# Subject products on pairs of tiles in quarters of TensorE, and routing in two batches: a mixture-of-experts kernel

## The chip, the cores and the metric

The kernel runs on one core of one Trainium2 chip. Its time is device microseconds from launch to end. The median of three runs of the kernel before is 865.85 us (863.19 to 867.67). One further execution was taken by the profiler; all rows below are from it.

## The reference

The input x is 64 samples of 64 rows and 512 columns. Each sample has a subject, one of 8.

```python
h = einsum('bct,bcd->bdt', x, weights[subjects]) + bias[subjects][:, :, None]  # 64x64 weights
tokens = h.reshape(4096, 512)
scores = sigmoid(tokens @ gate_weight.T)                  # 16 experts in 4 groups
biased = scores + expert_bias                             # best 2 of 4 groups, then best 4 experts
w = scores[chosen] / sum(scores[chosen]) * 2.5
y = sum over the 4 chosen experts of w * (silu(t @ g.T) * (t @ u.T) @ d.T)
out = x + y + the shared expert's (silu(t @ sg.T) * (t @ su.T) @ sd.T)
```

All is float32: h has 4096 tokens of 512 numbers, an expert 256 hidden units.

## The kernel before, in words

A tile is 128 tokens, that is two samples of 64 rows; there are 32. The program has a front stage and an expert stage. The expert stage runs 175 steps of one tile each: 32 for the shared expert, then 143 for the sorted tokens of the 16 experts. Each engine has its own list of instructions and waits on semaphores.

**The front stage.** ScalarE's queue (line 604) loads the first eight tiles of x into `x_ring`, and SyncE's queue (line 404) the later ones as slots come free; SyncE also stores each h tile to `h_rows` (line 411) and loads the shared expert's weights at tile 8. GpSimd (line 542) reads the two subjects of a tile and copies the two 64x64 weights into the diagonal quarters of a 128x128 block of `cw_ring`, whose other quarters were cleared at the start. TensorE (line 804) multiplies that block with the tile (line 812), then turns the h of the tile before with four transposes (line 768), and for each group of four tiles computes the router's logits in four column tiles of 32 (line 792) and turns them (line 802). The last four tiles' logits are computed directly, each tile in its turn (line 834). ScalarE adds the bias while it copies h out of PSUM (line 639), copies the transposes to a kept place (line 643), applies the sigmoid, and splits the shared weights in a high and a low part (line 620). VectorE routes in batches of eight tiles (`route_groups`, `top_experts`, `chosen_experts`, `count_slots`, `route_weights`): three batches before the expert stage, the fourth in its first steps. For each batch TensorE counts tokens ahead of each token (`positions`, line 771).

**Constants.** GpSimd builds them itself: `late_consts` (line 513) after the weights of tile 4, ending with `lane_q` and `tile_q`, and `clear_pads` (line 529) after tile 10 stores zeros behind `h_rows` and `out` with four DMAs.

**The order in the expert stage** is written out by hand in tables: ROUTE_STEPS says after which shared step VectorE does which part of the routing, ENTRY_STEPS when it builds the entries for the table of slots, PE_POS and PE_POS_FFN when TensorE does `positions`, RAW_LOADS, HIGHS and LOWS when weights are loaded and split, GATHERS when tokens are gathered. TensorE's step (line 920) is gate and up products of tile n, transposes of the hidden part of n - 1, a table or position product if one is due, and the down product of n - 2. At the end ScalarE copies the last three y tiles (line 747), and GpSimd scatters them.

Of the kernel before, what the change touches and what calls it, by code (L numbers as in the profile page):

```python
# [10 lines left out]
ALU = mybir.AluOpType  # L11
# [3 lines left out]
P = 128  # L15
B, C, H = 64, 64, 512
# [9 lines left out]
BC = 8  # L26
NB = NT // BC
BE = BC * E
# [28 lines left out]
ROUTE_STEPS = {0: ("groups",), 1: ("top_experts",), 2: ("ties", "counts"), 3: ("weights",), 4: ("ranks",),  # L57
               5: ("take_turns",), 6: ("starts",), 7: ("slots", "keys"), 8: ("top_slots",), 9: ("places",),
               10: ("words",), 11: ("columns",), 12: ("tables",), 14: ("read_words",), 15: ("read_sp_words",),
               22: ("fill_idx",)}  # L60
ENTRY_STEPS = {9: (0,), 11: (1,), 13: (2, 3), 14: (4,), 15: (5,), 16: (6, 7), 17: (8, 9), 18: (10, 11), 19: (12, 13),
               20: (14, 15)}
N_GROUPS = NT // ENTRIES
PE_POS = {18: 0, 26: 1}
PE_POS_FFN = {1: 2, 3: 3}
PE_WORDS = 13
PE_SP_WORDS = 14
SHARED_LOAD = 8
SHARED_HIGH = {16: 0, 19: 1, 22: 2}
PAD_STORES = 10  # L70
PAIR_TABLES = 4
# [3 lines left out]
HIGHS = {17: (1, 0), 18: (1, 1), 19: (1, 2), 24: (2, 0), 28: (2, 1), 31: (2, 2)}  # L75
# [7 lines left out]
FIRST_X_COPY = 30  # L83
# [21 lines left out]


def scored_by(tiles):

    if tiles <= DIRECT:
        return tiles // LOGIT_TILES  # L110
    return LOGIT_GROUPS + tiles - DIRECT
# [17 lines left out]
def build(nc, x, itok, fside, cond_w, gate_w, expert_bias, ffn_w, out):  # L129
# [4 lines left out]
    with ExitStack() as ctx:  # L134
# [80 lines left out]
        mask = in_raw([P, NB, NG + BC, E])  # L215
# [8 lines left out]
        ties = [in_raw([P, BC, BC + E]) for k in range(3)]  # L224
        top_ties = sb("top_ties", [P, BC, TOPK])
        n_ties = sb("n_ties", [P, BC])
        cum_part = [in_raw([P, NG + BC, E]) for k in range(2)]
# [72 lines left out]
        x_in = [sem(f"x_in{s}") for s in range(RING)]  # L300
# [71 lines left out]

        def shared_tile(n):

            return (n - KEPT_IN_X) % NT
# [10 lines left out]

        block = ctx.enter_context(nc.Block())

        @block.sync
        def _(sp):  # L390

            sp.dma_start(itok_row[:], itok.unsqueeze(0)).then_inc(itok_loaded, 16)
# [6 lines left out]
            def load_x(n):  # L399
                t = tile_at(n)  # L400
                sp.wait_ge(cond_done, t.done(1 - RING))
                sp.dma_start(x_ring[:, t.slot, :], rows(t, x_rows)).then_inc(x_in[t.slot], 16)

            for n in range(NT):
                t = tile_at(n)
                if n + RING < NT:
                    load_x(n + RING)
                if n == SHARED_LOAD:
                    sp.dma_start(raw_w[:, 0:EW], ffn_w[E]).then_inc(shared_loaded, 16)
                sp.wait_ge(h_ready, n + 1)  # L410
                sp.dma_start(rows(t, h_rows), tok_ring[:, t.slot, 0:H]).then_inc(h_stored[t.slot], 16)
# [81 lines left out]
        def _(pool):  # L493
# [19 lines left out]
            def late_consts():  # L513
# [10 lines left out]
                pool.sem_inc(consts, 1)  # L524
                iota(lane_q[:], [[1, P], [0, DUO]], 0, 0)
# [13 lines left out]
            pool.wait_ge(blank, 4)  # L539
            pool.wait_ge(itok_loaded, 16)  # L540

            for n in range(NT):
                subjects = [pool.value_load(itok_row[0:1, 2 * n + half:2 * n + half + 1]) & (NS - 1)
                            for half in range(2)]
                if n == 0:
                    pool.wait_ge(cond_loaded, 16)
                elif n >= RING:
                    pool.wait_ge(cond_done, n + 1 - RING)
                for half, subject in enumerate(subjects):
                    a, b = half * C, half * C + C  # L550
                    pool.tensor_copy(cw_ring[a:b, n % RING, a:b],
                                     cond_sb[a:b, bass.ds(subject * C, C)]).then_inc(cond_w_ready, 1)
                if n == PAIR_TABLES:
                    pool.wait_ge(cond_w_ready, 2 * (n + 1))
                    late_consts()
                elif n == PAD_STORES:
                    clear_pads()
# [45 lines left out]
        def _(act):  # L603
            for n in range(RING):
                if n == 2:
                    act.wait_ge(cond_loaded, 16)
                act.dma_start(x_ring[:, n, :], rows(tile_at(n), x_rows)).then_inc(x_in[n], 16)
# [24 lines left out]
            for n in range(NT + 2):  # L632
                t = tile_at(n)
                if n < NT:
                    act.wait_ge(cond_done, n + 1)
                    if n >= RING:
                        act.wait_ge(h_stored[t.slot], t.rnd * 16)
                        act.wait_ge(a_xposed, n + 1 - RING)
                    act.activation(tok_ring[:, t.slot, 0:H], psY[n % 2][:], ACT.Identity,
                                   bias=bias_tok[:, n:n + 1]).then_inc(h_ready, 1)  # L640
                if 1 <= n <= NT:
                    act.wait_ge(a_xposed, n)
                    act.activation(kept_xT(n - 1), psT[(n + 1) % 2][:], ACT.Copy).then_inc(a_xT_ready, 1)
# [13 lines left out]
                if n in SHARED_HIGH:  # L657
                    if SHARED_HIGH[n] == 0:
                        act.wait_ge(shared_loaded, 16)
                    split_high(0, SHARED_HIGH[n])  # L660
                elif n == FIRST_X_COPY:
                    copy_x(0)
# [836 lines left out]
```

## Time and profile before

| what | us |
|---|---|
| median of three runs | 865.85 |
| the profiled execution | 861.59 |
| its span, first to last instruction | 859.8 |
| start of the first expert product | 72.1 |
| TensorE busy | 838.1 |
| mean granted clock of TensorE | 0.992 of full |

The profiled execution's time is 1.8 us more than its span. In a view, "busy" is time with at least one instruction running on the engine, PEld is TensorE's loading of weights, and names ending in q are an engine's sequencer or queue.

### The profile page before, as it was taken

What the parts mean: (1) busy time and instruction counts of PE and PEld (TensorE: products, weight loads), DVE (VectorE), ACT (ScalarE), POOL (GpSimd) and SP (SyncE); (2) the same over time, 40 slices, a digit from 0 to 9 for tenths busy, and PEclk for the clock granted to TensorE, in tenths of its full rate; (3) what the DMA queues carried; (4) which work ended last, traced back from release to release, by engine and by line L of the source; (5) the groups of instructions that cost most, each with busy time, mean ns of one, the idle gap of its engine ahead of it and who ended that gap; (6) DMA issues with size and microseconds to landing.
All of it is one profiled execution on the core that took longest, in us unless ns stands there. A gap on an engine that the chain in (4) does not pass through costs nothing.

```text
span 859.8 us, 19571 instructions
## 1 busy us (share of the span) xinstructions
PE 838.1 (97%) x4151; PEld 675.4 (79%) x4152; DVE 485.0 (56%) x1055; ACT 418.1 (49%) x870; POOL 439.2 (51%) x402
## 2 busy tenths in 40 slices
PE   7999999999999999999999999999999999999994
PEld 5568887878888888888888888888887888887883
DVE  1478776564654444664446645756647466464440
ACT  3785355754543334644445444635445355453441
POOL 4430211143556555566665567566564665665433
PEclk8999999999999999999999999999999999999998
DMA  7994767579999999899998999899998999999644
GB/s 246 327 358 142 121 111 210 122 141 294 261 238 256 187 186 186 159 229 282 229 174 173 254 254 221 192 284 207 244 263 197 264 258 220 239 165 202 111 63 63
DMA packets 147097, 179.13 MB, mean 208 GB/s; under 512 B 30858, under 2 KB 104210, under 8 KB 144658
## 3 DMA queue, kind: packets, MB, share of 16 engines
q0 software_dynamic: 37296, 86.95, 50.9%
q1 hardware_dynamic: 108258, 80.45, 34.8%
q10 hardware_dynamic: 1408, 10.49, 3.7%
q14 instruction: 117, 0.96, 0.4%
q8 instruction: 18, 0.29, 0.2%
HBM read 82.52 MB, written 65.04 MB: 172 GB/s over the span
## 4 chain that ended last, share of the span: by engine, by line
PE 89%; issue 3%; ACT 3%; DVE 2%; DMA 1%; POOL 1%; DVEq 0%; ACTq 0%; SPq 0%
PE psGU L884 52%; PE psY L884 26%; PE psH L768 4%; PE psY L812 3%; PE psT L768 1%; DMA x_ring<-x 1%; PE psH L792 1%; ACT x_ring L712 1%; DVE entry L1291 1%; DVE x_ring L1293 1%; POOL out L567 1%; ACT split_w L620 0%; PE psGU L834 0%; ACT xT_hi L630 0%; PE psM L910 0%
## 5 line engine op out<-in xcount | busy, mean ns | idle before, releaser
L884 PE MATMUL psGU<-split_w,xT_hi 128*128 (+1 forms) x1400 | 432.0, 390 | 3.0 <-DVE xT_lo L1316 3.0
L567 POOL DMA_INDIRECT out<-y_ring,idx_all x143 | 234.0, 1636 | 205.0 <-SPq L471 189.2
L884 PEld LDWEIGHTS psGU<-split_w,xT_hi 128*128 128x128 f32 x1400 | 262.2, 188 | 60.2 <-issue 4.2
L884 PE MATMUL psGU<-split_w,xT_lo 128*128 (+1 forms) x700 | 273.4, 391 | 0.0
L884 PE MATMUL psY<-split_w,hidT_hi 128*128 (+1 forms) x700 | 232.5, 413 | 0.2 <-issue 0.2
L727 ACT ACTIVATE aT<-psGU 128x256 f32<-128x256 f32 x175 | 67.1, 384 | 259.4 <-PE psGU L884 259.4
L1316 DVE TENSOR_TENSOR xT_lo<-psT,xT_hi 128x512 fp32r<-128x512 f32 x143 | 98.8, 691 | 144.1 <-ACT xT_hi L630 128.3
L562 POOL DMA_INDIRECT tok_ring<-h_rows,idx_all x143 | 148.2, 1037 | 61.0 <-issue 42.7
L679 ACT ACTIVATE y_ring<-psY 128x512 f32<-128x512 f32 x175 | 103.7, 593 | 120.6 <-PE psY L884 115.2
L884 PEld LDWEIGHTS psGU<-split_w,xT_lo 128*128 128x128 f32 x700 | 131.4, 188 | 27.4
L884 PE MATMUL psY<-split_w,hidT_lo 128*128 (+1 forms) x350 | 137.5, 393 | 0.0
L884 PEld LDWEIGHTS psY<-split_w,hidT_hi 128*128 128x128 f32 x700 | 118.5, 189 | 16.1 <-issue 0.5
L1341 DVE SCALAR_TENSOR_TENSOR aT<-aT,w_ring,psGU 128x256 f32<-128x256 f32 x143 | 67.0, 469 | 87.4 <-ACT aT L727 87.3
L1323 DVE STREAM_TRANSPOSE psT<-x_ring 128x512 f32<-128x512 f32 x143 | 102.5, 717 | 0.0
L575 POOL DMA_DIRECT2D out<-y_ring x32 | 28.4, 902 | 113.6 <-ACT y_ring L679 113.3
L630 ACT ACTIVATE xT_hi<-psT 128x512 fp32r<-128x512 f32 x143 | 84.7, 592 | 1.7 <-DVE psT L1323 1.7
L884 PEld LDWEIGHTS psY<-split_w,hidT_lo 128*128 128x128 f32 x350 | 65.7, 188 | 14.4
L1356 DVE TENSOR_TENSOR split_w<-raw_w,split_w x42 | 51.5, 1227 | 42.4 <-ACT split_w L689 34.7
L1329 DVE TENSOR_TENSOR hidT_lo<-psH,hidT_hi 128x256 fp32r<-128x256 f32 x175 | 72.9, 417 | 1.0 <-ACT hidT_hi L670 1.0
L768 PEld LDWEIGHTS psH<-ident,aT 128*128 128x128 f32 x350 | 48.7, 140 | 24.0 <-DVE aT L1339 1.3
L768 PE MATMUL psH<-ident,aT 128*128 128x128 f32 x350 | 66.6, 271 | 0.5 <-DVE hidT_lo L1329 0.5
L670 ACT ACTIVATE hidT_hi<-psH 128x256 fp32r<-128x256 f32 x175 | 66.3, 379 | 1.4 <-PE psH L768 1.4
(184 smaller groups left out, 459.9 us busy)
## 6 DMA issues: line engine op xcount, KB each, us to landing
x_ring<-tok_ring SPq DMA_DIRECT2D x284, 128.0 KB
raw_w<-ffn_w SPq DMA_DIRECT2D x17, 1536.0 KB, 10.9
h_rows<-tok_ring SPq DMA_DIRECT2D x32, 256.0 KB, 6.8
out<-y_ring POOLq DMA_DIRECT2D x32, 256.0 KB
x_ring<-x SPq DMA_DIRECT2D x24, 256.0 KB, 7.8
tok_ring<-h_rows,idx_all POOLq DMA_INDIRECT x143, 6.4
out<-y_ring,idx_all POOLq DMA_INDIRECT x143
x_ring<-x ACTq DMA_DIRECT2D x8, 256.0 KB, 3.9
```

What stands on the lines that cost most here:

```text
L562: pool.indirect_dma_start(tok_ring[:, r % RING, :], None, h_rows[:, :], bass.IndirectOffsetOnAxis(idx_all[:, r:r + 1], 0)).then_inc(gather ...
L567: pool.indirect_dma_start(out[:, :], bass.IndirectOffsetOnAxis(idx_all[:, r:r + 1], 0), y_ring[:, r % YRING, :], None, compute_op=ALU.add) ...
L630: act.activation(xT_hi[:, t.slot % 2, :], xT, ACT.Copy).then_inc(xhi_ready, 1)
L670: act.activation(hidT_hi[:, t.slot % 2, :], psH[:, 0:I], ACT.Copy).then_inc(hidhi_ready, 1)
L679: act.activation(y_ring[:, s, :], psY[t.slot % 2][:], ACT.Copy).then_inc(y_ready, 1)
L727: act.activation(silu[:, t.slot % 2, :], psGU[t.slot % 2][:, 0:I], ACT.Silu).then_inc(silu_ready, 1)
L768: mm = pe.transpose(dst[:, k * P:(k + 1) * P], src[:, k * P:(k + 1) * P], ident[:])
L884: mm = pe.matmul(dst, a[:, slot, c], w(at + col + k * H), start=(k == 0 and a is high and at == 0), stop=(k == parts - 1 and a is low))
L1316: v.tensor_tensor(xT_lo[:, t.slot % 2, :], xT, xT_hi[:, t.slot % 2, :].bitcast(F32), ALU.subtract).then_inc(xT_ready, 1)
L1323: v.transpose(psT[t.slot % 2][:].rearrange("p (k b j) -> p k j b", k=HK, j=QUADS), x_duo[:, t.slot // DUO_TILES, :, t.slot % DUO_TILES, :] ...
L1329: v.tensor_tensor(hidT_lo[:, t.slot % 2, :], psH[:, 0:I], hidT_hi[:, t.slot % 2, :].bitcast(F32), ALU.subtract).then_inc(hidT_ready, 1)
L1341: ins = v.scalar_tensor_tensor(out=hid[:, half, :], in0=gate, scalar=w_ring[:, w_slot, bass.ds(expert, 1)], in1=up, op0=ALU.mult, op1=ALU. ...
```

## The change

- Tiles are handled in pairs. The four samples of a pair are loaded by two DMAs, samples 4m and 4m+3 into partitions 0 to 63, samples 4m+1 and 4m+2 into 64 to 127, each two slots wide.
- `cw_ring` holds each 64x64 weight once, in its first 64 columns, and is no longer cleared. TensorE does four products of 64 rows by 64 columns per pair, at four positions of its array. Four banks of PSUM take turns for h instead of two.
- VectorE copies the transposes of the first 16 tiles to their kept place; ScalarE those of the last 16.
- Routing has two batches of 16 tiles: the first before the expert stage, the second in shared steps 0 to 5. The running sums get one more stage and 8 columns of cleared lead. ROUTE_STEPS, ENTRY_STEPS, PE_POS, PE_POS_FFN and others move by about one step.
- The direct logits of the last four tiles come one after another behind the loop, with one sigmoid for all.
- The shared weights are loaded at pair 2 (tile 4), and split at pairs 6 to 8.
- `late_consts` comes after pair 7, `lane_q` and `tile_q` (now `entry_consts`) and `clear_pads` after the last pair.
- VectorE copies the third last y tile. The load of the subjects' numbers goes from SyncE's queue to ScalarE's.

```diff
-BC = 8
+BC = 16
+LEAD = 8
-PE_POS = {18: 0, 26: 1}
-PE_POS_FFN = {1: 2, 3: 3}
-SHARED_LOAD = 8
-SHARED_HIGH = {16: 0, 19: 1, 22: 2}
-PAD_STORES = 10
-PAIR_TABLES = 4
+PE_POS = {15: 0}
+PE_POS_FFN = {5: 1}
+SHARED_LOAD = 2
+SHARED_HIGH = {6: 0, 7: 1, 8: 2}
+PAIR_TABLES = 7
+DVE_COPIES = 16
-RAW_LOADS = {14: 1, 15: 2, 23: 3, 31: 4}
-WARM_UP = 12
+RAW_LOADS = {15: 1, 16: 2, 23: 3, 31: 4}
+WARM_UP = 8
-FIRST_X_COPY = 30
+FIRST_X_COPY = 15
...
+        def load_pair(eng, m):
+            at = m % X_PAIRS * 2
+            low, high = x[4 * m:4 * m + 4:3], x[4 * m + 1:4 * m + 3]
+            eng.dma_start(x_ring[0:C, at:at + 2, :], low.rearrange("b c t -> c b t")).then_inc(x_in[m % X_PAIRS], 16)
+            eng.dma_start(x_ring[C:P, at:at + 2, :], high.rearrange("b c t -> c b t")).then_inc(x_in[m % X_PAIRS], 16)
...
+        def h_bank(n):
+            return (psY if n // 2 % 2 == 0 else psGU)[n % 2]
...
+            for m in range(N_PAIRS):
+                if m + X_PAIRS < N_PAIRS:
+                    sp.wait_ge(cond_done, 2 * (m + 1))
+                    load_pair(sp, m + X_PAIRS)
+                if m == SHARED_LOAD:
                     sp.dma_start(raw_w[:, 0:EW], ffn_w[E]).then_inc(shared_loaded, 16)
+                for n in (2 * m, 2 * m + 1):
+                    t = tile_at(n)
+                    sp.wait_ge(h_ready, n + 1)
+                    sp.dma_start(rows(t, h_rows), tok_ring[:, t.slot, 0:H]).then_inc(h_stored[t.slot], 16)
...
+                    for half, subject in enumerate(subjects):
+                        a, b = half * C, half * C + C
+                        pool.tensor_copy(cw_ring[a:b, n % RING, 0:C],
+                                         cond_sb[a:b, bass.ds(subject * C, C)]).then_inc(cond_w_ready, 1)
+                if m == PAIR_TABLES:
+                    pool.wait_ge(cond_w_ready, 4 * (m + 1))
                     late_consts()
+            pool.wait_ge(cond_w_ready, 2 * NT)
+            entry_consts()
+            pool.wait_ge(blank, 3)
+            clear_pads()
...
+            for m in range(N_PAIRS + 1):
+                pair = (2 * m, 2 * m + 1)
+                if m < N_PAIRS:
+                    for n in pair:
+                        copy_h(n)
+                if 2 * m > DVE_COPIES:
+                    for n in pair:
+                        keep_xT(n - 2)
...
+            def cond(m):
+                at = m % X_PAIRS * 2
+                pe.wait_ge(x_in[m % X_PAIRS], (m // X_PAIRS + 1) * 32)
+                if m >= 2:
+                    pe.wait_ge(h_ready, 2 * (m - 1))
+                for k, (n, rows_at, cols_at) in enumerate(((2 * m, 0, 0), (2 * m, C, C), (2 * m + 1, 0, C), (2 * m + 1, C, 0))):
...
+                    mm = pe.matmul(h_bank(n)[cols_at:cols_at + C, :], cw_ring[rows_at:rows_at + C, n % RING, 0:C],
+                                   x_ring[rows_at:rows_at + C, at + n % 2, :], start=True, stop=True,
+                                   tile_position=(rows_at, cols_at))
+                    if k % 2 == 1:
+                        mm.then_inc(cond_done, 1)
...
+            for m in range(N_PAIRS + 1):
+                if m < N_PAIRS:
+                    cond(m)
+                if m == 0:
                     bias()
...
+                if m >= 1:
+                    for n in (2 * m - 2, 2 * m - 1):
+                        turn_h(n)
...
+            for n in range(DIRECT, NT):
+                mm = direct_logits(n)
+            mm.then_inc(logits_done, 1)
...
-            v.memset(cw_ring[:], 0.0).then_inc(blank, 1)
...
+            for n in range(DVE_COPIES):
+                v.wait_ge(a_xposed, n + 1)
+                v.tensor_copy(kept_xT(n), psT[n % 2][:]).then_inc(a_xT_ready, 1)
```

## Rows read from the trace of the kernel before

**Rows 1.** The page's part 1: busy us, share of the span, instructions.

```profile
PE 838.1 (97%) x4151; PEld 675.4 (79%) x4152; DVE 485.0 (56%) x1055; ACT 418.1 (49%) x870; POOL 439.2 (51%) x402
```

**Rows 2.** Waits of TensorE, whole span: us in total, times, longest us.

```profile
PE psY L812 <- issue: 3.7, 1, 3.7
PE psGU L884 <- DVE xT_lo L1316: 3.0, 3, 1.6
...
PE psY L812 <- DMA x_ring<-x: 1.2, 1, 1.2
```

**Rows 3.** Timeline of TensorE: start us, us, line, what; products and transposes of tiles.

```profile
30.98 1.02 PE L812 MATMUL psY<-x_ring,cw_ring 128*128 128x512 f32 x2
31.85 0.60 PE L768 MATMUL psT<-ident,tok_ring 128*128 128x128 f32 x4
32.28 1.02 PE L812 MATMUL psY<-x_ring,cw_ring 128*128 128x512 f32 x2
...
72.10 0.72 PE L884 MATMUL psGU<-split_w,xT_hi 128*128 128x512 f32 x2
```

**Rows 4.** Chain that ended last: a logit group, and one tile's direct logits.

```profile
28.54 1.01 PE psH L792 x32
...
71.19 1.06 PE psGU L834 x8
```

**Rows 5.** Groups of ScalarE, 0 to 72 us: busy us, mean ns, idle before.

```profile
L639 ACT ACTIVATE tok_ring<-psY,bias_tok 128x512 f32<-128x512 f32 x32 | 22.0, 689 | 14.8 <-PE psY L812 12.3 <-issue 1.1
L643 ACT ACTIVATE kept_w<-psT 128x512 f32<-128x512 f32 x24 | 14.3, 595 | 0.3 <-PE psT L768 0.2
...
L620 ACT ACTIVATE split_w<-raw_w 128x1024 fp32r<-128x1024 f32 x3 | 3.2, 1061 | 0.0
L647 ACT ACTIVATE logitsT<-psH 128x128 f32<-128x128 f32 x7 | 1.9, 277 | 2.8 <-PE psH L792 2.7
```

**Rows 6.** Stretches of the front: engines' busy us, TensorE's clock, DMA share, GB/s.

```profile
core 0: us, PE busy (x) PEld busy (x) DVE busy (x) ACT busy (x) POOL busy (x), PEclk, DMA share, GB/s
...
40.00:60.00 20.00, 18.43 (x169) 11.21 (x168) 14.39 (x53) 15.70 (x30) 9.07 (x26) 1.00 1.05 400
...
17.00:23.70 6.70, 6.10 (x40) 3.51 (x41) 0.00 (x0) 1.56 (x3) 3.33 (x13) 0.50 0.36 123
```

**Rows 7.** DMA issues, 0 to 72 us: count, KB each, us to landing.

```profile
x_ring<-x SPq DMA_DIRECT2D x24, 256.0 KB, 7.8
```

**Rows 8.** Timeline of GpSimd: constants, and copies of subject weights.

```profile
9.36 0.29 POOL L515 TENSOR_SCALAR_AFFINE_SELECT before<-ones 128x128 f32<-128x128 f32 x1
...
13.17 1.68 POOL L507 IOTA tile_q<- 128x288 f16 x1
16.98 0.52 POOL L551 COPY cw_ring<-cond_sb 64x64 f32 x2 [2.13 <-issue]
18.00 0.52 POOL L551 COPY cw_ring<-cond_sb 64x64 f32 x2 [0.50 <-issue]
```

**Rows 9.** VectorE: groups by form, then the first batch's first and last operation.

```profile
L967 DVE TENSOR_TENSOR raw_w<-raw_w 128x128 f32<-128x128 f32 x24 | 7.0, 290 | 0.7
...
L1316 DVE TENSOR_TENSOR xT_lo<-x_ring,xT_hi 128x512 fp32r<-128x512 f32 x2 | 1.3, 684 | 0.0
...
L1339 DVE TENSOR_TENSOR aT<-aT,psGU 128x256 f32<-128x256 f32 x32 | 13.3, 417 | 5.7 <-ACT aT L727 5.3
...
32.06 0.29 DVE L967 TENSOR_TENSOR masked<-scores,ebias 128x128 f32<-128x128 f32 x1 [21.31 <-ACT scores L650]
...
41.70 0.23 DVE L1096 TENSOR_SCALAR weights_te<-w_num 128x128 f32<-128x128 f32 x1
```

**Rows 10.** A stretch of the expert stage with 32-partition transfers; columns as in rows 6.

```profile
240.80:242.15 1.35, 1.35 (x8) 1.12 (x7) 1.04 (x2) 0.28 (x1) 0.00 (x0) 1.00 1.20 189
```

**Rows 11.** Timeline of the end: y copy by ScalarE, first of the last three scatters.

```profile
845.68 0.59 ACT L679 ACTIVATE y_ring<-psY 128x512 f32<-128x512 f32 x1
...
846.58 1.56 POOL L567 DMA_INDIRECT out<-y_ring,idx_all  x1 [3.33 <-SPq L471]
```

More of the change, by code:

```diff
@@ L537, in clear_pads @@
                                    ).then_inc(scattered[2 * k + 1], 16)
-            pool.wait_ge(blank, 4)
             pool.wait_ge(itok_loaded, 16)
[L542 to L554, printed above, removed]
+            for m in range(N_PAIRS):
+                for n, first, second in ((2 * m, 4 * m, 4 * m + 1), (2 * m + 1, 4 * m + 3, 4 * m + 2)):
+                    subjects = [pool.value_load(itok_row[0:1, b:b + 1]) & (NS - 1) for b in (first, second)]
+                    if n == 0:
+                        pool.wait_ge(cond_loaded, 16)
+                    elif m >= X_PAIRS:
+                        pool.wait_ge(cond_done, 2 * (m + 1 - X_PAIRS))
+                    for half, subject in enumerate(subjects):
[4 more added lines that the diff above has]
+                    pool.wait_ge(cond_w_ready, 4 * (m + 1))
                     late_consts()
-                elif n == PAD_STORES:
-                    clear_pads()
+            pool.wait_ge(cond_w_ready, 2 * NT)
+            entry_consts()
+            pool.wait_ge(blank, 3)
+            clear_pads()
             def gather(r):
@@ L603, in _ @@
         def _(act):
-            for n in range(RING):
-                if n == 2:
+            act.dma_start(itok_row[:], itok.unsqueeze(0)).then_inc(itok_loaded, 16)
+            for m in range(X_PAIRS):
+                if m == 1:
                     act.wait_ge(cond_loaded, 16)
-                act.dma_start(x_ring[:, n, :], rows(tile_at(n), x_rows)).then_inc(x_in[n], 16)
+                load_pair(act, m)
             act.wait_ge(blank, 2)
@@ new lines, in turn_h, with direct_logits @@
+            def turn_h(n):
+                pe.wait_ge(h_ready, n + 1)
+                if n >= 2:
+                    pe.wait_ge(a_xT_ready, n - 1)
+                transposes(psT[n % 2], tok_ring[:, n % RING, 0:H], HK).then_inc(a_xposed, 1)
+            def direct_logits(n):
+                pe.wait_ge(a_xT_ready, n + 1)
+                at = (n - DIRECT) * E
+                xT = kept_xT(n)
+                for k in range(HK):
+                    mm = pe.matmul(psY[0][:, at:at + E], xT[:, k * P:(k + 1) * P], gate_sb[:, k * Q:k * Q + E],
+                                   start=(k == 0), stop=(k == HK - 1))
+                return mm
@@ L837, in _ @@
-                if n in PE_POS:
-                    positions(PE_POS[n])
+                elif 1 <= g <= LOGIT_GROUPS and phase == 0:
+                    turn_logits(g - 1)
+                if m in PE_POS:
+                    positions(PE_POS[m])
+            for n in range(DIRECT, NT):
+                mm = direct_logits(n)
+            mm.then_inc(logits_done, 1)
             def word_tables():
@@ L1025, in route_groups, with best_groups @@
                 settle()
+            def best_groups(b):
+                four = masked[:].rearrange("p (g j) -> p g j", j=GS)
                 sums = per_chunk(group_sum[:], NG)
@@ L1372, in route_part @@
                         route_groups(NB - 1)
+                    elif part == "best_groups":
+                        best_groups(NB - 1)
                     elif part == "top_experts":
@@ L1431, in step @@
                     next_weights(word)
+            for j in range(PIECES):
+                split_low(0, j)
             route_groups(0)
+            best_groups(0)
             top_experts(0)
```

199 lines of the change are left out of this document (77 added, 122 removed).

## The prediction

> **What bounds the kernel now.** I read the busy times of the page first: TensorE is busy 97% of the span and every other engine about half [rows 1]. The table of waits then tells where TensorE stands still: 3.7 us once before a subject product, 1.2 us for a tile of x, 3.0 us in three waits for VectorE's `xT_lo`, and nothing else of size [rows 2]. So the expert stage from 72.1 us on is TensorE's own work, and the change leaves that work as it is. What it rebuilds is the front stage, 0 to 72.1 us, where the first expert product starts: 8% of the span [rows 3].
>
> In the front three things run side by side. TensorE: in a stretch with no waits a subject product takes 31.85 - 30.98 = 0.87 us and the four transposes of a tile 32.28 - 31.85 = 0.43, so 1.30 a tile [rows 3]; a group of four tiles' logits takes 1.01 [rows 4]. With 0.3 around it, four tiles are 6.5 us. ScalarE: 0.69 for the copy of h, 0.60 for the kept transpose, 1.29 a tile, plus 3.2 us of weight splitting and some 0.5 per four tiles for logits, of which 0.27 is the copy shown [rows 5]; it is as full as TensorE. DMA: from 40 to 60 us the engines are full (share 1.05, 400 GB/s) [rows 6], because x (8.39 MB) comes in, h (8.39 MB) goes out and weights (1.57 MB) and pads (2.13 MB) lie between; a load landed 7.8 us after its issue [rows 7].
>
> The 72.1 us are then: 8.1 until the second tile's product, 31 more tiles at 1.63 = 50.5, the direct logits 4 x about 1.0 = 4 [rows 4], sum 62.6. The other 9.5: GpSimd builds constants from 9.36 to 14.85 and gives the sixth tile's weights only at 16.98, so TensorE waits 3.7 [rows 2, 8]; after that wait its granted clock is 0.50 of full (1.2 instead of 2.4 GHz) from 17.0 to 23.7 [rows 6], which costs about 6.7 / 2 = 3.3; 1.2 is the wait for x [rows 2]; 1.3 remain, for ScalarE's three splits of 1.06 [rows 5] and two position products.
>
> **The change part by part.**
> *Products.* Before, two tiles cost 2 x 0.87 = 1.74. After, there are four products of 64 rows by 64 columns, each with the same 512 moving columns, so 4 x 0.87 = 3.5 one after another. How far they overlap is the question. The nearest row is the logit group: 32 passes of 128 columns in 1.01 us, where transposes do four such passes in 0.43, so 32 in 3.5; four column tiles side by side ran 3.4 times as fast [rows 3, 4]. No row shows row tiles. Bounds for a pair: 0.87 + 0.2 for the change of shape on each side = 1.1, and 3.5 + 0.3 = 3.8. I take 1.2, nearest to the logit group. (The Trainium skill, TensorEngine Tiling (Array Packing), Restrictions and Gotchas, says row tiles may not use one PSUM bank at once. Here the two row tiles of one column half go to different banks, but the diagonal pair shares one. By that rule, read strictly, a pair takes 2 x 0.87 + 0.3 = 2.0, which is a rival below.)
>
> *TensorE's pair.* 1.2 + 8 transposes 0.87 + half a logit group with its change of shape and turn 0.66 + 0.25 for waits on ScalarE = 3.0, where it was 3.25. ScalarE: the first eight pairs 2 x 0.69 + 0.25 = 1.6, later 2 x 1.29 + 0.25 = 2.85. VectorE: a copy of 128x512 out of PSUM costs about as `xT_lo`, 0.68 [rows 9], 1.4 a pair; its larger clearings (ties twice as long) make it ready near 12 us, 1 us late for the third pair.
>
> *Constants.* late_consts moves from tile 4 to pair 7, the two long iotas (1.53, 1.68) behind the last pair. GpSimd needs 1.02 a tile [rows 8], so it is ahead of TensorE's 1.5 a tile: by pair 7 its lead covers 2.2 us of iotas, even with a 2.1 us pause like the one behind tile_q. The 3.7 wait and the 3.3 of slow clock go (bounds 0 and 7). The pads (4 stores, 2.1 MB) leave the front; they are wanted only before the first y copy, 13 us into the next stage.
>
> Without any DMA limit: third pair's end at 13.7 (8.6 for the first product and h, two pairs without logits at 2.1, 1 for VectorE), 13 pairs x 3.0 = 39, positions of 16 tiles 1.0, last transposes 0.9, ScalarE's order (two h, two kept, x_hi for the first two tiles, two kept) 1.3, four direct logits 3.8: expert stage at 59.7.
>
> *The loads of x.* This is where I expect the gain to shrink. Each pair now comes as two DMAs into 64 partitions each, one behind the other in one queue, and all 16 engines serve each. The trace has full-width traffic at 400 GB/s with share 1.05, but in 240.80 to 242.15 us, where almost only `x_ring<-tok_ring` transfers into 32 partitions run, the share is 1.20 and only 189 GB/s move [rows 10]. Their packets are smaller (512 B), so part of that is size. Bounds for a load of x: 400 GB/s (1.31 us a pair) and 189 (2.77). I take 250 (2.1 us), because the small packets explain some of the row. The last load of x stands behind 15 pairs of loads and 11 pairs of stores of h: 16 x 2.1 + 11 x 1.31 + weights 1.57 MB at 400 GB/s 3.9 [rows 6] + start and small loads 4.0 = 55.9 us. From its landing: product 1.2, ScalarE's 6.3 (two h, two kept, logit copy, issue of copy_x, two x_hi, two kept), last direct logits 1.1: 64.5. DMA thus outlasts TensorE's 59.7 by 5 us. At 400 the landing is 43.3 + 8.6 = 52, hidden; at 189 it is 66.6 and the stage starts at 75.2.
> (The Trainium skill, SBUF — State Buffer, Door 1, says partitions 0 to 63 reach only 8 of 16 DMA ports, 196 GB/s against 328 measured there, asymptote 218, and that two DMAs for the two halves gain 6% together, not twofold. The window of [rows 10] agrees in direction. By 218 my sum would be 60.7 + 8.6 = 69.3, an estimate from that page.)
>
> *Routing in two batches of 16.* VectorE's step of one batch is a chain of some 40 operations: one of 128x128 is 0.29, of 128x256 0.42; a batch of 8 took 32.06 to 41.93, 9.9 us [rows 9]; one of 16 comes to about 15.4 (some 20 long operations +0.13 each, 8 more MAX at 0.09, one more step each for ties and counts). Batch 0 starts with the fourth logit group near 37 us, has its counts at 50 and ends at 52.5: TensorE wants the counts at 52 or later. Hidden, with 2 us of cover; if gone, as many us. Batch 1 now lies in shared steps 0 to 5 with at most 3.3 us of routing beside 0.68 + 0.42 + 0.42 of its own [rows 9], in a step of (848.6 - 72.1) / 175 = 4.4 with 848.6 as TensorE's end; TensorE uses the result one step later, so an overrun of 0.5 is covered by the next product. I take 0, bounds -1 and +4. TensorE's position products: four of 0.8 become two of about 1.1; two leave the expert stage and one comes, -0.4.
>
> *End.* VectorE copies the third last y right after its product: ScalarE did it 845.68 to 846.27, in its turn [rows 11]; now about 845.0 to 845.7. GpSimd's last three scatters follow one another from there: -0.6.
>
> Sum for the forecast: 64.5 - 72.1 = -7.6, -0.4, -0.6: -8.6. The profiled execution took 861.6 (span 859.8 and 1.8 around it), 4.2 below the median of 865.85 (863.2 to 867.7); it becomes 853.0, and the median 857.3.
>
> **Rivals.**
> A. Loads are not slowed by the halves: stage at 59.7, -13.4, median 852.5. For it: a 512 B shuffle is a poor witness for 2 KB rows. Against: share 1.20 means the engines were full and still slow.
> B. The halves cost fully (189 to 220 GB/s, 2.4 to 2.8 us a pair): stage at 69 to 75, -4 to +2, median 862 to 868. For it stand [rows 10]; against it, that loads alternate with stores of h, which spread over all partitions.
> C, the slower one: as B at 189, and TensorE starves during the weight load, because one queue carries both. The load of 1.57 MB stands between two pairs; a wait like the 3.7 us before 17.6 brings the clock to 1.2 GHz for 6.7 us again, +3.3: 78.5, +5.4, median 871. It decides once a load of x takes 2.6 us a pair or more.
> D. Quarters don't overlap: 3.8 instead of 1.2 a pair gives 13 x 5.6 + 5 more at the start: stage near 98, +25, median 891. With only two at a time (2.0) the pair is 3.8: stage near 71, median 864.
>
> **Numbers.** Forecast 35%, A 27%, B 20%, C 8%, D 10% (half of it two at a time). About 0.5% (4.3 us) is what a measurement of this kernel tells from no change. Faster: forecast and A, and B's upper end, 66%. Same: most of B and half of D, 20%. Slower: C, the other half of D and B's lower end, 14%. Range 848 to 869: it holds A with 4 us of spread and C's edge, and leaves out D and the tails.
>
> **What would show it.** The first expert product's start is the main reading (64.5; 59.7 in A; 69 or later in B). The four products: eight passes within about 1.0 us, or 1.9, or 3.5. The DMA row: GB/s from 20 to 50 us at a share above 1 is near 300 in the forecast, near 400 in A, near 260 in B; TensorE waits for x_ring by DMA some 5 us in total, none in A. The granted clock stays 1.00 through 17 to 24 us. Waits of TensorE for VectorE past the front stay near 3 us. The prediction is wrong if the front is set by ScalarE or VectorE, if TensorE waits for `cum`, or if the expert stage takes another length than 787.

## The result: 1.4% slower, though the front stage gained 9 us

The changed kernel takes 878.3 us (median of 4 runs, 875.8 to 881.8) where the kernel before, beside it, takes 866.8 (863.2 to 868.4): ratio 1.0142, interval 1.0093 to 1.0190. The forecast was 857.3 with a range of 848 to 869. The profiled execution has a span of 877.0 us, against 859.8 before. The chain that ended last, between 56 and 70 us, and the page's part 1 (order as in [rows 1]):

```profile
56.85 0.43 DVE raw_w L1119
57.42 0.67 PE psM L798 x2
58.09 0.43 PE psM L799 x2
...
59.50 3.48 PE psY L854 x32
62.98 7.17 PE psGU L923 x24
```

```profile
PE 843.0 (96%) x4199; PEld 673.5 (77%) x4200; DVE 486.0 (55%) x1003; ACT 407.5 (46%) x850; POOL 441.8 (50%) x402
```

The first expert product (`psGU` of L923) starts at 62.8 us, 9.3 before that of [rows 3] (the chain, which follows matmuls' ends, puts it at 63.0). So the front did a little better than forecast (64.5), and everything after it took 814.2 us and not 787.7: 26.5 us longer. The waits of TensorE, VectorE and ScalarE over the whole span say by whom (columns as in [rows 2]):

```profile
PE psGU L923 <- DVE xT_lo L1357: 10.1, 6, 3.7
PE psGU L923 <- issue: 4.7, 1, 4.7
PE psGU L835 <- DMA x_ring<-x: 3.0, 1, 3.0
```

```profile
DVE xT_lo L1357 <- ACT xT_hi L638: 135.5, 94, 3.4
DVE aT L1382 <- ACT aT L746: 66.2, 68, 3.5
DVE xT_lo L1357 <- issue: 62.1, 36, 7.3
```

TensorE's wait for VectorE's `xT_lo` is 10.1 us where it was 3.0 [rows 2]. VectorE itself waits 62.1 us for "issue", nothing that the profile shows, ahead of `xT_lo`. In the kernel before that line was:

```profile
DVE xT_lo L1316 <- issue: 15.5, 18, 4.7
```

To find where, I took the start of ScalarE's activation `aT<-psGU` of each of the 175 tiles from the two traces and subtracted. "Tile 21" is the last at which the shared tiles are still mixed with routing work; the loop's six turns that follow lie at tiles 64, 80, 96, 112, 128 and 144.

```
stretch                                before     after    difference
first expert product                    72.10     62.83      -9.3
 from it to tile 0's activation          3.06      4.55      +1.5  (clock at 1.2 GHz, 64.0 to 67.4)
 tile 0 to 21, shared                  102.70    108.19      +5.5
 tile 21 to 64                         186.03    186.78      +0.8
 tile 64 to 174                        479.50    498.77     +19.3
 from there to the end                  16.45     15.86      -0.6
```

In the last long stretch nearly all tiles take 4.34 us in both kernels, and the large exceptions come once in sixteen: tiles 64, 80, 96, 112, 128 and 144 take 5.35, 4.65, 8.65, 9.89, 10.87 and 6.39, which is 19.8 us above six ordinary ones. In the kernel before those six take 4.33 to 4.42. VectorE's timeline around the third turn, changed kernel, then before:

```profile
499.26 0.48 DVE L1382 SCALAR_TENSOR_TENSOR aT<-aT,w_ring,psGU 128x256 f32<-128x256 f32 x1 [0.82 <-ACT aT L746]
499.65 0.42 DVE L1370 TENSOR_TENSOR hidT_lo<-psH,hidT_hi 128x256 fp32r<-128x256 f32 x1
506.13 0.69 DVE L1357 TENSOR_TENSOR xT_lo<-psT,xT_hi 128x512 fp32r<-128x512 f32 x1 [6.06 <-issue]
```

```profile
498.77 0.48 DVE L1341 SCALAR_TENSOR_TENSOR aT<-aT,w_ring,psGU 128x256 f32<-128x256 f32 x1 [0.80 <-ACT aT L727]
499.17 0.42 DVE L1329 TENSOR_TENSOR hidT_lo<-psH,hidT_hi 128x256 fp32r<-128x256 f32 x1
500.88 0.69 DVE L1316 TENSOR_TENSOR xT_lo<-psT,xT_hi 128x512 fp32r<-128x512 f32 x1 [1.29 <-ACT xT_hi L630]
```

Between `hidT_lo` and `xT_lo` the changed kernel's VectorE stands 6.06 us. TensorE, one tile ahead, then stands too, and its granted clock falls (stretches, columns as in [rows 6]):

```profile
507.01 0.73 PE L923 MATMUL psGU<-split_w,xT_hi 128*128 x2 [2.43 <-DVE xT_lo L1357]
```

```profile
505.00:508.00 3.00, 0.99 (x4) 0.81 (x5) 1.87 (x4) 0.72 (x2) 2.17 (x2) 0.95 1.13 290
508.00:511.00 3.00, 3.00 (x9) 2.35 (x8) 1.47 (x3) 0.09 (x1) 0.46 (x1) 0.50 1.14 270
```

TensorE's waits at the six turns are 0.7, 0, 2.4, 3.7, 4.7 and 1.8 us, 13.3 in sum (the 4.7 is the row "issue" above). Behind the third, fourth and fifth its clock is at 0.50 for 3.4 us each, in which it does half the work, 1.7 us lost each time. The two make 18.4 of the 19.8 us.

The trace also records the sequencer's own instructions. There most of the 6 us is one gap: after the compare-and-branch that closes VectorE's loop, the first instruction of the loop's next turn, a branch hint, comes 5.16 us later. The gaps of all six turns:

```
VectorE, us from the branch back to the loop's first instruction
before   0.48  0.50  0.46  0.48  0.47  0.50
after    1.19  2.58  5.16  6.39  5.05  1.48
```

### The profile page after: what moved, and what is told of

Its sections match the earlier page's. It is cut to its first block, busy times and chain, and to the rows that moved or that the text cites. A ratio compares the mean times of both kernels' runs of the same rounds, so it can differ in the third digit from the quotient of the medians.

```text
span 877.0 us, 19572 instructions
## 1 busy us (share of the span) xinstructions
PE 843.0 (96%) x4199; PEld 673.5 (77%) x4200; DVE 486.0 (55%) x1003; ACT 407.5 (46%) x850; POOL 441.8 (50%) x402
## 4 chain that ended last, share of the span: by engine, by line
PE 81%; issue 6%; DVE 6%; ACT 3%; DMA 1%; DVEq 1%; SPq 0%; POOL 0%; ACTq 0%
PE psGU L923 50%; PE psY L923 24%; PE psH L788 4%; DMA x_ring<-x 1%; DVE xT_lo L1357 1%; ACT x_ring L731 1%; PE psT L788 1%; PE psY L835 1%; ACT xT_hi L638 1%; PE psGU L835 1%; ACT y_ring L698 1%; DVE x_ring L1334 1%; PE psM L774 0%; DVE hidT_lo L1370 0%; PE psY L854 0%
## 5 line engine op out<-in xcount | busy, mean ns | idle before, releaser
L923 PE MATMUL psGU<-split_w,xT_hi 128*128 (+1 forms) x1400 | 439.3, 395 | 14.8 <-DVE xT_lo L1357 10.1
L574 POOL DMA_INDIRECT out<-y_ring,idx_all x143 | 236.4, 1653 | 223.3 <-SPq L474 205.1
L923 PEld LDWEIGHTS psGU<-split_w,xT_hi 128*128 128x128 f32 x1400 | 265.8, 190 | 75.1 <-issue 17.5
L923 PE MATMUL psGU<-split_w,xT_lo 128*128 (+1 forms) x700 | 276.5, 395 | 0.0
L923 PE MATMUL psY<-split_w,hidT_hi 128*128 (+1 forms) x700 | 233.8, 415 | 0.2 <-issue 0.2
L923 PEld LDWEIGHTS psGU<-split_w,xT_lo 128*128 128x128 f32 x700 | 133.2, 190 | 29.5
L923 PE MATMUL psY<-split_w,hidT_lo 128*128 (+1 forms) x350 | 138.5, 396 | 0.0
L923 PEld LDWEIGHTS psY<-split_w,hidT_hi 128*128 128x128 f32 x700 | 119.0, 190 | 16.5 <-issue 0.5
L923 PEld LDWEIGHTS psY<-split_w,hidT_lo 128*128 128x128 f32 x350 | 65.9, 188 | 15.3
```

The lines of the kernel that those rows point to most:

```text
L574: pool.indirect_dma_start(out[:, :], bass.IndirectOffsetOnAxis(idx_all[:, r:r + 1], 0), y_ring[:, r % YRING, :], None, compute_op=ALU.add) ...
L923: mm = pe.matmul(dst, a[:, slot, c], w(at + col + k * H), start=(k == 0 and a is high and at == 0), stop=(k == parts - 1 and a is low))
```

## Experiments on the loop's turn

The loop is the same in both kernels. What differs is where it stands in VectorE's program: by the program's listing it begins with instruction 1114 before and with 1059 after, because the routing in two batches is shorter by 55 instructions. (The traces number nothing, but the loop's first branch hint is the 710th instruction recorded for VectorE before and the 655th after, 55 apart.) The trace's DMA records have packets of instructions, most of 8 KB. I took 128 instructions to such a packet; the second test below checks that. The tests move the loop with semaphore increments that nothing waits for (`PAD` of them):

```
+                if n is not None and NT <= n < NT + 15:
+                    for k in range(PAD // 15 + (n - NT < PAD % 15)):
+                        v.sem_inc(spare, 1)
```

**The changed kernel, 55 increments.** 

> The kernel after with 55 more instructions on VectorE, semaphore increments that nothing waits for, spread over the 15 routed tiles ahead of its loop. VectorE's loop then begins at the same instruction of its program (number 1114) as in the kernel before, where after it begins at number 1059; nothing else differs. Theory 'place of the loop': after loses 19 us because VectorE stands 1.2, 2.6, 5.2, 6.4, 5.1 and 1.5 us behind the branch at the loop's end, where the kernel before stands 0.5 us each time, and this depends on where the loop stands in the program. It expects the six waits at 0.5 us, steps of 4.35 us there, and a median 17 to 20 us under that of after: 858 to 862 us, faster than before by 5 to 9 us. Rival 'traffic': the waits come from what the DMA queues carry in that stretch, which the front's new timing has shifted; it expects the waits to stay between 1 and 6 us and the time within 3 us of 878. Rival 'less slack': the waits are there in both kernels and after has less cover; excluded if the six waits change.

Measured: all six gaps 0.46 to 0.50 us; 862.2 us, ratio to before 0.9982 (0.9953 to 1.0010). The changed kernel's ratio was 1.0142, so 55 idle instructions win 1.6%, 14 us. (The medians differ by 16, but the kernel before, too, was 4 us faster beside this one: 862.6 against 866.8.) The gaps went as expected; the gain on the kernel before that I had expected with them, 5 to 9 us, did not come.

**The kernel before, 73 increments.** 

> The kernel before with 73 such increments on VectorE, so that its loop begins at number 1187, which is 128 instructions (8 KB, the size of one instruction packet in the trace) behind the 1059 of after. Theory 'place of the loop', with the packets of 8 KB as its period: this kernel gets the six waits of after, and a median of 880 to 887 us, 15 to 20 us over that of before (866). If the place matters but with another period: anything from 866 to 887. Rival 'traffic': the front and the transfers are those of before, so the waits stay 0.5 us and the time within 2 us of 866.

Measured: gaps of 1.19, 3.60, 5.01, 5.71, 4.06 and 1.27 us; 879.7 us, ratio 1.0221 (1.0168 to 1.0273). The kernel before gets the whole loss, with its own front, transfers and routing, and it gets it 128 instructions behind the place in the changed kernel (1187 and 1059). Its VectorE, at the third turn:

```profile
501.33 0.41 DVE L1331 TENSOR_TENSOR hidT_lo<-psH,hidT_hi 128x256 fp32r<-128x256 f32 x1
507.66 0.69 DVE L1318 TENSOR_TENSOR xT_lo<-psT,xT_hi 128x512 fp32r<-128x512 f32 x1 [5.91 <-issue]
```

The two together settle it: the place of VectorE's loop is the cause, and the rivals "traffic" and "less slack" fall. That it repeats after 128 instructions, the length of a packet, speaks for the fetching of instructions, which no test here moves by itself.

**The changed kernel, 27 increments.** 

> The kernel after with 27 such increments, half way (its loop begins at number 1086). Theory 'place of the loop': either the waits go in steps with the place, then one between those of after (22 us in sum) and those of before (3 us), some 860 to 878 us, or there is an edge and the time is one of the two. Rival 'traffic': 875 to 881 us.

**The same, timed.** 

> The kernel with 27 idle increments again (VectorE's loop begins at number 1086), now timed, as the base of the next three, whose loops are set to the same place. Its one run gave 859.2 us. Theory: with the waits at the loop's turns gone, what is left of the change is the front's gain of 9 us less what the shared stage gives back, 3 to 5 us: ratio to before 0.993 to 0.998 (857 to 861 where before is 863). Rival 'nothing is left': 1.000 and more.

Measured: 859.2 us in the single run, then 862.8, ratio 0.9975 (0.9946 to 1.0003). The gaps are 0.5 us but for the third and fourth, 1.6 and 1.6, then 2.5 and 1.5: the wait goes in steps. Gaps of this size cost nothing here, tiles 96 and 112 take 4.35 us in both traces. The first expert product came at 62.6 in the timed kernel's trace and tile 21 at 171.0, against 177.9 before.

**The changed kernel, 73 increments.** 

> The kernel after with 73 idle increments: VectorE's loop begins at number 1132 and its branch back is at 1795, 3 instructions into a packet of 128 (58 in after, 85 with 27 increments, 113 in before). Theory 'the end's place in its packet': what counts is how many instructions of its last packet VectorE passes before it branches back, since the packet of the loop's head is fetched meanwhile; 3 is the worst case, with six waits of 3 to 8 us and 880 to 900 us. Theory 'the head's place': the head is 108 into its packet, further than in before, so the waits stay 0.5 us and the time 858 to 863 us. Rival 'traffic': 878 us.

Measured: all gaps 0.49 to 0.50 us and 865.8 us (its front ended late, at 67.8). The theory "the end's place" called this the worst case and was wrong here; "the head's place" had the gaps right.

What the gaps wait for can be read from the instruction packets in the DMA records. They don't say for which engine they are, so this is by their times:

```
VectorE        gap, and start of the nearest packet, both from the branch (us)
after          1.19 -0.6 | 2.58 +0.6 | 5.16 +3.2 | 6.39 +4.4 | 5.05 +2.6 | 1.48 -0.6
before+73      1.19 -0.6 | 3.60 +1.8 | 5.01 +3.2 | 5.71 +3.5 | 4.06 +1.9 | 1.27 -0.5
after+27 timed 0.49 -2.4 | 0.50 -1.5 | 2.50 +0.7 | 1.52 -0.6 | 0.47 -2.7 | 0.49 -1.9
before         0.48 -6.7 | 0.50 -5.9 | 0.46 -4.9 | 0.48 -5.2 | 0.47 -6.1 | 0.50 -5.5
```

Where VectorE stands, it goes on 1.8 to 2.5 us after a packet starts; where the packet starts 1.5 us or more ahead of the branch, the gap is 0.5. Set in order by where the loop's last instruction stands in its packet of 128, the longest gaps in all the traces are:

```
place of the branch back     3    20    58    69     85   86   94   113  123-124
engine                      DVE   SP   DVE   ACT    DVE  ACT  ACT   DVE   SP
longest gap, us             0.5   5.2   6.4  2.5    2.7  2.0  0.4   0.5  0.2-0.7
```

The values of 20 and 94 come from the kernel with halves of single tiles, below, the 2.7 at 85 from the one with twelve warm-up products. The places are counted in the program's listing, and no trace shows where a packet begins. So the distances between VectorE's four places (27, 28 and 18 instructions) are sure, the places themselves and the comparison of one engine with another are not. VectorE's columns would fit a fetch of the loop's head that is asked for at a fixed point of each packet, so that the branch comes too early when it follows soon behind. That is inferred, not shown.

Two engines are poor witnesses. TensorE shows 0.06 us between its branch and the loop's first instruction, at every turn of every kernel. The packets of 16 KB, 18 in all, have a queue of their own and none starts between 340 and 835 us, in which TensorE goes back seven times: if they are TensorE's, it keeps its loop and fetches nothing at a turn. SyncE's 5.2 us came in the kernel in which 97 packets of 8 KB start from 350 to 770 us, where the kernel before has 68: it seems to fetch its loop at each turn there, and in the other kernels not. Why the gaps grow and shrink over the six turns stays open.

## Experiments on the shared stage and the front

All four of the next kernels have VectorE's loop begin at 1086, as the kernel with 27 increments.

**One-hot tables ahead of the routing part.** In steps 10 to 16 VectorE did its routing part, then the tables; now the other way round.

```
+                if n != FIRST_ENTRY:
+                    for g in ENTRY_STEPS.get(n, ()):
+                        make_entries(g)
                 for part in ROUTE_STEPS.get(n, ()):
...
-                for g in ENTRY_STEPS.get(n, ()):
-                    make_entries(g)
```

> The kernel with 27 idle increments, and VectorE makes the one-hot tables of a shared tile (ENTRY_STEPS) ahead of its routing part and not behind it (but for the first, which needs the places just made). Theory 'chain through ScalarE': in the steps 10 to 16 VectorE goes from its routing part to the tables, ScalarE scales them and only then copies the next tile of x to its high half, for which VectorE waits 1.74 us in each such step; a step so lasts 2.9 us plus the routing part and the tables, 6.6 us in steps 11 and 13. With the tables first, ScalarE scales them beside the routing part: the steps 11, 12 and 13 fall by 1 to 2 us each, the stretch from tile 0 to tile 21 from 105.3 to 101 to 103 us, the whole by 2 to 4 us. Rival 'VectorE's sum of work bounds the stretch': no change, 105 us, within 1 us of the base. Rival 'TensorE waits for the tables instead': slower by 1 us.

Measured: step 11 falls from 6.45 to 4.89 us, step 13 from 6.64 to 4.91, step 12 stays at 5.2, step 14 rises from 5.88 to 7.09; tile 0 to 21 takes 102.8 and not 105.3; 857.7 us, ratio to before 0.9948 (0.9919 to 0.9978). VectorE's end of step 11, first the kernel with 27 increments, then this one:

```profile
118.68 0.68 DVE L1336 TENSOR_TENSOR x_ring<-lane_q,slot_lane 128x1024 f16<-128x1024 f16 x1
119.28 0.42 DVE L1382 TENSOR_TENSOR aT<-aT,psGU 128x256 f32<-128x256 f32 x1
119.61 0.42 DVE L1372 TENSOR_TENSOR hidT_lo<-psH,hidT_hi 128x256 fp32r<-128x256 f32 x1
121.76 0.69 DVE L1359 TENSOR_TENSOR xT_lo<-kept_w,xT_hi 128x512 fp32r<-128x512 f32 x1 [1.74 <-ACT xT_hi L640]
```

```profile
114.72 0.68 DVE L1337 TENSOR_TENSOR x_ring<-lane_q,slot_lane 128x1024 f16<-128x1024 f16 x1
115.32 0.41 DVE L1223 TENSOR_REDUCE e_rows<-cw_ring 128x16 f32<-128x256 f32 x1
...
118.02 0.42 DVE L1373 TENSOR_TENSOR hidT_lo<-psH,hidT_hi 128x256 fp32r<-128x256 f32 x1
118.36 0.68 DVE L1360 TENSOR_TENSOR xT_lo<-kept_w,xT_hi 128x512 fp32r<-128x512 f32 x1
```

The table comes last in the first fence, ScalarE scales it before it copies `xT_hi`, and VectorE waits 1.74 us. In the second, 2.4 us of routing lie behind the table and the wait is gone. The bound was a chain VectorE, ScalarE, VectorE; VectorE's sum of work is the same in both.

**The same with VectorE's loop at 1114.** 

> The kernel that makes the tables first, with 55 idle increments and not 27: VectorE's loop begins at number 1114. Theory 'place of the loop': at 1086 two of its six waits at the loop's turn are 0.9 to 2.7 us long and hidden (VectorE runs ahead of TensorE), at 1114 all are 0.5 us; the time is that of the base within 1 us or 1 us less: 855 to 858 us where before is 863 to 865, ratio 0.991 to 0.995. This is the version that should beat both kernels. Rival 'only 1086 is good': ratio over 0.998.

Measured: all gaps 0.46 to 0.50; 860.1 us, ratio 0.9939 (0.9911 to 0.9966). This version, as the one above, beats both kernels. The two are not told apart.

**Twelve warm-up products, and all early copies by ScalarE,** two kernels:

```
-WARM_UP = 8                -DVE_COPIES = 16
+WARM_UP = 12               +DVE_COPIES = 0
```

> The kernel with 27 idle increments, and WARM_UP 12 as in the kernel before in place of 8. In after TensorE runs at 1.2 GHz to 16.2 us, in before it does not. Theory 'the loads set the front': the first expert product comes within 0.5 us of the base (63 to 65.5 us in the two traces so far). Rival 'the late clock costs the front': 1 to 3 us earlier.

Measured: first product at 63.5, 860.4 us. No gain; the late clock at the start is hidden.

> The kernel with 27 idle increments, and ScalarE makes all copies of turned tiles (DVE_COPIES 0), as in the kernel before, where VectorE made the first 16. Theory: the first half of the front is then ScalarE's, with 2 copies of x by 0.55 us in each pair of 5.2 us: a pair takes ScalarE 0.64 + 0.64 + 0.55 + 0.55 + 0.3 + 0.24 us, 3 us, and the front stays within 1 us (ScalarE has room). Rival 'ScalarE is full': the first expert product 3 to 9 us later (16 copies by 0.59 us).

Measured: first product at 63.8, 858.8 us. ScalarE has room, and with VectorE's copies the front is not measurably shorter.

**Quarter products twice.**

```
+                for turn in range(2):
                     for k, (dst, w, rhs, at) in enumerate(quarters):
                         mm = pe.matmul(dst, w, rhs, start=True, stop=True, tile_position=at)
```

> The kernel with 27 idle increments, and each of the quarter products is issued twice (the second writes the same result), so that a pair of tiles has 8 matmuls and takes TensorE 2.0 us and not 1.02 us at 2.4 GHz. Theory 'TensorE sets the front from 30 us on': of the 16 pairs the last 10 or 11 run without a wait for anything, so the first expert product comes 10 to 11 us later, 73 to 75 us, and the earlier pairs hide theirs in the waits for x. Rival 'loads or the routing chain set the front': 63 to 66 us as in the base, or 1 to 5 us later. What that tells: a pair of tiles by the products of the kernel before (4.1 us a pair) would cost the front 30 us more in place of 10.

TensorE's timeline, one pair's products:

```profile
38.28 1.95 PE L843 MATMUL psGU<-x_ring,cw_ring 64*64 64x512 f32 x16
```

Measured: 16 passes in 1.95 us, first product at 68.4, 3.5 to 5.8 us later than the bases' 62.6 to 65.0. I expected 10 to 11, and the rival 1 to 5: the number is nearer to the rival's. It is also close to the 67.8 of the kernel with 73 increments, whose front has no work added, so one trace hardly tells a price. The wait for x of 3.0 us is down to 0.2, and here the chain that ended last runs on TensorE without a break from 31.4 us to the first expert product. In the changed kernel that chain runs through VectorE's routing from 45 to 57 us, and in the kernel with 27 increments through a load of x until 56, so part of the doubled work could hide there. (It took 871.4 us, more than its front explains; 485.9 of it in tiles 64 to 174, where other runs had 480 to 488.)

**x in halves, in the kernel before.**

```
-                sp.dma_start(x_ring[:, t.slot, :], rows(t, x_rows)).then_inc(x_in[t.slot], 16)
+                for a in (0, C):
+                    sp.dma_start(x_ring[a:a + C, t.slot, :], rows(t, x_rows)[a:a + C, :]).then_inc(x_in[t.slot], 16)
```

> The kernel before, each tile of x loaded by two DMAs of 64 partitions (as the change does) in place of one of 128. Only the front is of interest: the added DMA issues on SyncE and ScalarE also move their loops. Theory 'halves cost next to nothing beside stores': x's tiles land within 0.5 us of the 7.8 us they take in before, the rate from 20 to 50 us stays 350 to 400 GB/s, the first expert product stays at 71 to 73 us. Rival 'a half reaches half of the paths to memory': the rate falls toward 250 GB/s and the first expert product comes 3 to 10 us later.

Measured: first product at 77.8, 5.7 us later, 875.0 us. Taken alone this spoke for the rival, but the edit also doubles the DMA issues: ScalarE issues until 12.0 us. SyncE's loop moved too (gaps to 5.2 us). So a second kernel keeps the number of issues:

**x in halves of pairs, in the kernel before.** 

> The kernel before, with x loaded as the change does: two DMAs of 64 partitions for each pair of tiles, each half of both tiles (256 KB a DMA, as before), so that there are as many issues as in before and all loops stay at their places. Each pair is loaded once both its slots are free, one tile later than before. Theory 'halves cost next to nothing': the DMAs land in 4 to 8 us, the rate from 20 to 50 us is 350 to 400 GB/s once stores run beside them, the first expert product comes at 71 to 74 us and the kernel takes 861 to 868 us; the 5.7 us that the doubled count of DMAs cost the kernel with halves of single tiles came from the 11.2 us that ScalarE took to issue 16 of them and SyncE's 0.6 us for each more. Rival 'a half reaches half of the paths': the early rate (0 to 30 us) falls by a fifth and more, the first product comes at 76 us or later.

```
-                sp.dma_start(x_ring[:, t.slot, :], rows(t, x_rows)).then_inc(x_in[t.slot], 16)
+                for a in (0, C):
+                    load_half(sp, n, a)      # partitions a to a + 63 of tiles n and n + 1
```

Measured: first product at 72.5 (72.1 before), 860.7 us in one run, where the kernel before took 864.8 in one. Stretches of it, columns as in [rows 6]:

```profile
10.00:20.00 10.00, 6.29 (x40) 3.81 (x44) 0.89 (x6) 6.67 (x13) 6.16 (x15) 1.00 1.07 256
20.00:30.00 10.00, 10.00 (x102) 6.26 (x91) 0.18 (x1) 7.42 (x17) 5.81 (x16) 1.00 0.96 303
30.00:40.00 10.00, 8.51 (x65) 4.84 (x64) 8.81 (x42) 6.07 (x12) 2.73 (x10) 1.00 1.02 383
```

Beside stores the engines move 383 GB/s from 30 to 40 us. But the 0.4 us are not the price of the halves. TensorE's clock is 1.00 in every stretch of this front, where the kernel before runs at 0.50 from 17.0 to 23.7 us behind its wait of 3.7 [rows 6], and the last load of x lands at 62.5 us and not at 60.2. So a loss in the loads and a gain in the clock cancel, and what the halves cost alone is not shown.

Early in the front, where loads of x are most of the traffic, halves are slower. Stretches of the changed kernel, then of the kernel before:

```profile
7.50:10.00 2.50, 2.50 (x16) 1.02 (x12) 0.00 (x0) 1.42 (x2) 1.05 (x5) 1.00 1.06 239
10.00:15.00 5.00, 5.00 (x24) 2.08 (x24) 4.50 (x14) 2.53 (x4) 1.93 (x9) 1.00 1.05 236
```

```profile
7.50:10.00 2.50, 2.34 (x12) 1.43 (x12) 1.56 (x7) 2.44 (x4) 1.42 (x7) 1.00 0.98 294
10.00:15.00 5.00, 3.94 (x19) 2.12 (x17) 0.74 (x6) 4.12 (x7) 4.34 (x7) 1.00 1.01 360
```

In all four the DMA engines are busy throughout (share 0.98 to 1.06); with halves they move 239 and 236 GB/s, with full height 294 and 360. (The second stretch has the first stores of h in both kernels, four and five issues.) The kernel with halves of pairs moves 252 and 224 in the same two stretches.

## Why the prediction was wrong, by its steps

- **"The expert stage from 72.1 us on is TensorE's own work, and the change leaves that work as it is."** This step failed. The work is nearly the same, but its length was not 787: 814. Of the 26.5 us, 19.3 lie in tiles 64 to 174, at the loop's turns, where VectorE stands up to 6.4 us between its branch and the next instruction. Shown both ways: 55 instructions added to the changed kernel take the gaps away, 73 added to the kernel before bring them. That the gap is a wait for the loop's instructions to arrive is inferred from the packets' times. The prediction counted operations and never where the code stands. The 15.5 us of `xT_lo <- issue` before would not have told it: with all gaps at 0.5 us the kernel with 55 increments still has 14.7.
- **"Routing: I take 0, bounds -1 and +4."** Mis-sized. Tile 0 to 21 is 5.5 us longer; 2.6 where the clock stays up (the timed kernel with 27 increments), the rest where it falls. In the changed kernel it does, for 6.8 us from 132.2 on, after a stretch in which TensorE was busy 4.09 of 5 us:

```profile
125.00:130.00 5.00, 4.09 (x18) 3.00 (x16) 4.72 (x14) 1.24 (x4) 0.80 (x1) 1.00 0.35 54
130.00:135.00 5.00, 4.74 (x31) 3.44 (x32) 3.27 (x7) 3.52 (x8) 0.84 (x1) 0.72 0.81 241
135.00:140.00 5.00, 5.00 (x15) 3.96 (x14) 2.73 (x8) 2.56 (x5) 0.85 (x1) 0.59 0.30 36
```

  I had compared the routing part with the room in a step (3.3 us) and left out ScalarE's share of the chain: with a table at its end, a step lasts about 2.9 us plus routing and table.
- **Products, 1.2 us a pair.** Right, 1.02: of a pair's eight passes four start within 0.02 us, the other four 0.48 us later, and the next work follows 1.02 us after the first (1.98 at 1.2 GHz). The timeline's row for one pair:

```profile
19.96 1.09 PE L835 MATMUL psY<-x_ring,cw_ring 64*64 64x512 f32 x8
```

  The Trainium skill, TensorEngine Tiling (Array Packing), Restrictions and Gotchas, says that row tiles can't use one PSUM bank at the same time. By that rule read strictly, the pair would take the 2.0 us of the prediction's rival. No such cost shows here, though the diagonal pair writes one bank, each of the two its own half of the partitions.
- **Loads of x, 250 GB/s.** Right where they run nearly alone, 236 to 239 GB/s from 7.5 to 15 us; beside stores, from 30 us on, 386 to 389 GB/s moved, and a pair's loads and stores came every 2.8 us, forecast 2.1 + 1.31 = 3.4. The sum still came out, because the loads wait for free slots: the last one landed at 52.6 us in the changed kernel and at 54.1 to 57.7 in its five variants whose chain runs through a late load of x (27, 27 timed, 55 and 73 increments, twelve warm-up products), forecast 55.9. The first expert product followed 8.5 to 10.1 us behind it there, forecast 8.6. TensorE's wait for x was 3.0 us, and 4.7 to 7.0 in those five, forecast 5. The chain of the kernel with 27 increments:

```profile
46.70 9.43 DMA x_ring<-x
56.17 1.09 PE psGU L837 x8
```

  The Trainium skill, SBUF — State Buffer, Door 1, gives 64 partitions half the ports. The early stretches agree in direction, 239 against 294 GB/s at a DMA share near 1; from 30 us on, where the two halves travel one behind the other and beside stores, nothing of that size is seen.
- **Constants.** The 3.7 us wait went. The slow clock did not go, it moved: 1.2 GHz to 16.2 us and, behind the wait for x, from 29.8 to 36.7. Twelve warm-up products changed nothing.
- **"Counts at 50, TensorE wants them at 52, 2 us of cover."** The batch began at 45.1 and not 37, when ScalarE's scores of the 16th tile came (VectorE had stood 2.2 us for them); counts at 57.3. TensorE, later too, waited 0.2 us. The cover was nearly zero, and in the changed kernel the chain that ended last runs through VectorE's routing from 45.05 to 57.28 us, one of the prediction's own signs of being wrong. That the changed kernel's front came near its forecast (62.8 against 64.5) is so in part luck: in five traces of the same front work it took 62.6 to 67.8 us, and now the loads, now the routing came last.
- **End, -0.6.** Right, 0.6 measured.
- The rivals B, C and D are out, and none had the true cause. A's start of the expert stage (59.7) is further from the measured 62.8 than the forecast's 64.5. C's "slower" came for another reason.

With the loop at a good place the changed kernel is 0.18% to 0.25% faster than before, no change by the bound of 0.5%: a front shorter by 9 pays for the routing pushed into the shared steps. What is left open: the 0.02 us that each unrolled tile of 21 to 64 takes more (0.8 us in all), and 4 to 7 us in tiles 126 to 139 that the traces of five kernels with small VectorE gaps lose (27 timed, 55, tables first at 1114, quarters twice, halves of single tiles) and the other kernels without long gaps hardly; two executions of the kernel with 27 increments differ in just this.

## What to carry to other kernels

When a kernel has loops too long to keep, note for each engine where the loop stands before and after an edit, and compare the loop's turns before anything else: "issue" waits that come once a turn may be instructions arriving late, and a few idle ones ahead of the loop may be worth more than the edit. Time saved ahead of a stage is only kept if what was moved into that stage fits its longest chain over all engines, not just the free time of one.

## What the runs showed of the hardware

- A wrong place of VectorE's loop cost gaps of up to 6.4 us a turn, 14 us in all in one kernel (ratio 1.0142 against 0.9982) and 2.2% in the other. The gaps come back when the loop is moved by 128 instructions, and end 1.8 to 2.5 us after an 8 KB packet of instructions starts. ScalarE and SyncE show the same kind of gap (to 2.5 and 5.2 us); TensorE shows 0.06 us at every turn.
- Four 64x64 products of fp32 with 512 moving columns run beside one another, two of them into one PSUM bank: 1.02 us for eight passes.
- Loads of x into 64 partitions moved 239 GB/s with the DMA engines full, where full height moved 294; with stores beside, 386 to 389. With the same number of issues the front was 72.5 against 72.1 us, though with a better clock; with twice the issues it was 5.7 us longer.
